# A Mamba and mixture-of-experts layer on one core: two sums of h*C in place of one, three buffers of h, and some steps moved

## The reference

```python
h = layernorm(x) * (1 + ca) + sa
z = h @ W_in;  val, gate = split(z)
val = silu(conv3(val))                      # depthwise over tokens, 3 taps, zero padding
B, C = val @ W_B, val @ W_C                 # 16 states
Delta = softplus((val @ W_delta + base) @ W_tau)
dA = Delta * A;  A_bar = exp(dA);  B_bar = expm1(dA) / (dA + 1e-6) * Delta * B
h_t = A_bar_t * h_{t-1} + B_bar_t * val_t   # for each of 512 channels and 16 states
y_t = sum over states of h_t * C_t
x = x + ga * (y * silu(gate) @ W_out + h)
h = layernorm(x) * (1 + cb) + sb
x = x + gb * (sum over the top 2 of 8 experts of gate_e * expert_e(h) + shared(h))
```

## Time and profile before

| | us |
|---|---|
| median of 3 runs | 4693.78 (4690.15 to 4694.49) |
| profiled execution | 4706.26 |
| its span in the trace | 4704.5 |
| granted TensorE clock, mean of the span | 0.887 |

### The profile page before, as it was taken

How to read it: one execution, slowest core, us unless ns; L and a number is a source line. 1 busy time by engine, 2 the same in 40 slices (tenths; PEclk the granted TensorE clock), 3 DMA queues, 4 the chain that set the end, 5 groups by cost and what they waited for, 6 DMA issues and landing times.

```text
span 4704.5 us, 37136 instructions
## 1 busy us (share of the span) xinstructions
PE 3843.4 (82%) x9708; PEld 1610.7 (34%) x9708; DVE 4026.5 (86%) x3880; ACT 3975.7 (85%) x4410; POOL 3647.9 (78%) x2304
## 2 busy tenths in 40 slices
PE   6624423999898989999899999999899977988889
PEld 3201101334333333333333333333333333333344
DVE  1388799999999999999999999999999987887820
ACT  2688889998989898999989899989999897887811
POOL 0389988887889888888889888888898886767721
PEclk8856656999999999999999999999999988989889
DMA  4588867889888888888888888888888876657542
GB/s 133 204 237 264 235 168 201 237 237 256 236 243 235 256 243 262 228 250 253 238 253 231 253 236 256 235 265 231 249 253 236 239 207 167 188 156 196 151 132 67
DMA packets 352221, 1037.19 MB, mean 220 GB/s; under 512 B 41253, under 2 KB 44389, under 8 KB 344710
## 3 DMA queue, kind: packets, MB, share of 16 engines
q1 hardware_dynamic: 278282, 766.35, 47.9%
q0 software_dynamic: 73728, 268.47, 28.8%
HBM read 639.74 MB, written 126.51 MB: 163 GB/s over the span
## 4 chain that ended last, share of the span: by engine, by line
ACT 20%; PE 19%; issue 15%; POOL 14%; DMA 13%; DVE 10%; SPq 0%; POOLq 0%; DVEq 0%; ACTq 0%
DMA ysum<-hs 11%; PE ps L1129 7%; PE ps L1148 6%; POOL inv L1390 4%; PE ps L1099 4%; ACT inv L761 3%; POOL hs L1363 3%; ACT th L772 3%; ACT inv L754 2%; ACT inv L767 2%; DVE ps L1195 2%; ACT abar L776 2%; DVE ps L1189 2%; DVE ps L1183 2%; POOL ysum L1377 2%
## 5 line engine op out<-in xcount | busy, mean ns | idle before, releaser
L1390 POOL TENSOR_TENSOR inv<-inv,th 128x1024 f32<-128x1024 f32 x512 | 1270.5, 2481 | 153.1 <-ACT th L772 153.0
L1129 PE MATMUL ps<-hf,w1r 128*128 128x512 f32 x2304 | 1129.7, 644 | 99.6 <-DMA w1r<-in_W 60.5
L1363 POOL TENSOR_TENSOR hs<-hs,Cb 128x1024 f32<-128x1024 f32 x384 | 979.7, 2551 | 28.9 <-DVE hs L1213 12.3
L1148 PE MATMUL ps<-w2r,hid 128*128 128x512 f32 x1776 | 818.3, 608 | 0.1
L1166 PE MATMUL ps<-Brow,pick 48*128 48x512 bf16 x1024 | 341.2, 416 | 576.6 <-DVE hs L1213 575.6
L1183 DVE SCALAR_TENSOR_TENSOR ps<-ps,us 128x1024 f32<-128x1024 f32 x512 | 627.8, 1226 | 172.3 <-PE ps L1166 171.8
L1377 POOL DMA_DIRECT2D ysum<-hs x480 | 443.1, 923 | 376.3 <-DMA ysum<-hs 367.2
L754 ACT ACTIVATE inv<-nrd,kappa 128x1024 f32<-128x1024 f32 (+1 forms) x640 | 578.1, 968 | 175.5 <-DVE ps L1195 171.4
L1129 PEld LDWEIGHTS ps<-hf,w1r 128*128 128x128 f32 x2304 | 458.9, 206 | 690.0 <-issue 640.9
L1202 DVE SCALAR_TENSOR_TENSOR ps<-nrd,inv_kappa,ps 128x1024 f32<-128x1024 f32 (+1 forms) x640 | 674.9, 1073 | 15.8
L1213 DVE TENSOR_TENSOR_SCAN hs<-abar,carry,ps 128x512 f32<-128x512 f32 (+1 forms) x384 | 683.1, 1800 | 0.3
(11 more groups left out here) (155 smaller groups left out, 5014.4 us busy)
## 6 DMA issues: line engine op xcount, KB each, us to landing
ysum<-hs POOLq DMA_DIRECT2D x512, 512.0 KB, 5.6
Cb<-c_rows SPq DMA_DIRECT2D x384, 512.0 KB, 4.6
w1r<-in_W SPq DMA_DIRECT2D x144, 512.0 KB, 5.6
w2r<-w_scaled SPq DMA_DIRECT2D x141, 512.0 KB, 7.3
Cb<-c_rows SPq DMA_DIRECT2D x128, 256.0 KB, 3.9
gbc<-expert_gates SPq DMA_DIRECT2D x128, 256.0 KB, 5.2
aw<-in_W_val SPq DMA_DIRECT2D x64, 256.0 KB, 6.3
xa<-in_x SPq DMA_DIRECT2D x32, 512.0 KB, 7.6
```

What stands on the lines that cost most here:

```text
L1129: mm = t.matmul(o, w1r[:, n % 2, k, h * P:(h + 1) * P], hf[:, k, :], start=(k == 0), stop=(k == G - 1))
L1148: mm = t.matmul(o, hidden(e)[:, h, tt * P:(tt + 1) * P], (last_w2(e) if q == NQ - 1 and grp == 1 else w2r[:, e % 3])[:, h, :], start=(grp ...
L1363: gp_.tensor_tensor(hs[:, c % 4, :], hs[:, c % 4, :], Cb[:, c % 2, :], ALU.mult).then_inc(hC_done, 1)
L1390: gp_.tensor_tensor(inv[:, c % 6, :], inv[:, c % 6, :], th[:, c % 3, :], ALU.mult).then_inc(thinv_done, 1)
```

## The change

It has eight parts.

1. `ysum` gets two tiles: even states add to the one, odd states to the other, each with a semaphore of its own. A sum now waits for the one two states before.
2. `add_to_y(c - 1)` stands right behind `times_C(c - 1)`, ahead of everything else of POOL's slot, but for r = 1 and 17, where it stays last.
3. `gate_y` adds the two tiles (a new POOL instruction, 128 x 1024) before it multiplies by the gate.
4. `hs` has three buffers in place of four; the scan of c waits for the sum of c - 3.
5. The edge columns of the convolution: ACT evicts all 512 columns in one activation, and DVE adds the neighbours' values with one `tensor_tensor` per block on a strided view (128 x 4 x 2), behind the four convolutions. The Silu waits for it.
6. At r = 3 DVE runs the fourth convolution ahead of the add of an expert sum (L1252) and not behind it.
7. SP loads expert p = 8 (`load_w1(qf, 8)`) at r = 23 in place of 24.
8. SP loads the gated y of a block at r = 2 in place of 3, but for the last four blocks.

```diff
-        hs = sb("hs", [P, 4, TB])
-        ysum = sb("ysum", [P, TB])
+        hs = sb("hs", [P, 3, TB])
+        ysum = sb("ysum", [P, 2, TB])
...
-            if r == 3 and has(qf):
+            if r == (2 if qf < NQ - 4 else 3) and has(qf):
                 sp.wait_ge(gy_st, 16 * units_before_end(qf))
                 ge(sp, f_gates, qf)
                 sp.dma_start(gyin, ...).then_inc(gy_ld, 16)
...
-            if r == 24:
+            if r == 23:
                 load_w1(qf, 8)
...
-                        s.activation(uu[:, m, 1:T - 1], o[:, 1:T - 1], ACT.Identity, scale=middle).then_inc(ev_val, 1)
-                        s.activation(uu[:, m, 0:1], o[:, 0:1], ACT.Identity, scale=middle,
-                                     bias=vhalo[:, m, q:q + 1]).then_inc(ev_val, 1)
-                        s.activation(uu[:, m, T - 1:T], o[:, T - 1:T], ACT.Identity, scale=middle,
-                                     bias=vhalo[:, m, NQ + q:NQ + q + 1]).then_inc(ev_val, 1)
+                        s.activation(uu[:, m, :], ps[:, bank_of["val", q, m], :], ACT.Identity,
+                                     scale=tapc[:, 1, m:m + 1]).then_inc(ev_val, 1)
...
             def silu_of_u(q):
-                    act.wait_ge(conv_done, G * (q + 1))
+                    act.wait_ge(edges_done, q + 1)
...
-                    if c >= 4:
-                        dve.wait_ge(y_summed, 16 * (c - 3))
+                    if c >= 3:
+                        dve.wait_ge(y_summed[(c - 3) % 2], 16 * ((c - 3) // 2 + 1))
...
             def late():
+                if r == 3:
+                    convolve(qa, 3)
                 if r in (2, 3, 4, 5):
                     add_x1("w2", qp, 12 * qp + 8 + r - 2, mm_w2, ev_w2)
-                if r == 3:
-                    convolve(qa, 3)
+                if r == 3 and has(qa):
+                    dve.wait_ge(conv_done, G * (qa + 1))
+                    ends = uu[:, :, 0:T:T - 1]
+                    v.tensor_tensor(ends, ends, vhalo[:, :, qa:NQ + qa + 1:NQ], ALU.add).then_inc(edges_done, 1)
...
             def add_to_y(c):
                     pool.wait_ge(hC_done, c + 1)
-                    if c % N == 0:
+                    if c % N < 2:
                         ge(pool, y_gated, unit(c))
-                        gp_.dma_start(ysum[:], hs[:, c % 4, :]).then_inc(y_summed, 16)
+                        gp_.dma_start(ysum[:, c % 2, :], hs[:, c % 3, :]).then_inc(y_summed[c % 2], 16)
                     else:
-                        pool.wait_ge(y_summed, 16 * c)
-                        gp_.dma_start(ysum[:], hs[:, c % 4, :], accum_op=ALU.add).then_inc(y_summed, 16)
+                        pool.wait_ge(y_summed[c % 2], 16 * (c // 2))
+                        gp_.dma_start(ysum[:, c % 2, :], hs[:, c % 3, :], accum_op=ALU.add).then_inc(y_summed[c % 2], 16)
...
             def gate_y(u):
-                    pool.wait_ge(y_summed, 16 * N * (u + 1))
+                    for odd in range(2):
+                        pool.wait_ge(y_summed[odd], 16 * (N // 2) * (u + 1))
+                    gp_.tensor_tensor(ysum[:, 0, :], ysum[:, 0, :], ysum[:, 1, :], ALU.add).then_inc(y_joined, 1)
+                    pool.wait_ge(y_joined, u + 1)
                     pool.wait_ge(gate_ld, 16 * (u + 1))
-                    gp_.tensor_tensor(gy[:], ysum[:], gy[:], ALU.mult).then_inc(y_gated, 1)
+                    gp_.tensor_tensor(gy[:], ysum[:, 0, :], gy[:], ALU.mult).then_inc(y_gated, 1)
...
             times_C(c - 1)
+            if r not in (1, 17):
+                add_to_y(c - 1)
...
             weight(c + 2)
             if r in (1, 17):
                 gate_y(c // N - 1)
-            add_to_y(c - 1)
+                add_to_y(c - 1)
```

More of the change, by code:

```diff
@@ L386, in adaln_mamba_moe @@
             sem("B_ready"), sem("uB_done"), sem("abar_plus_1_done"), sem("weighted_done"), sem("bu_done"), sem("scan_done"))
-        y_summed, y_gated, carry_done = sem("y_summed"), sem("y_gated"), sem("carry_done")
+        y_summed = [sem("even_states_summed"), sem("odd_states_summed")]
+        y_joined, y_gated, carry_done = sem("y_joined"), sem("y_gated"), sem("carry_done")
         a_stat, a_log, a_rstd, a_shift, a_xn = (
             sem("a_stats"), sem("a_log_variance"), sem("a_rstd"), sem("a_shift"), sem("a_normalized"))
-        tap_left, conv_done, b_split = sem("tap_left"), sem("conv_done"), sem("b_split")
+        tap_left, conv_done, edges_done, b_split = sem("tap_left"), sem("conv_done"), sem("conv_edges_done"), sem("b_split")
         ax_ld = [sem("a_x_loaded_0"), sem("a_x_loaded_1")]
@@ L846, in take_val @@
                         act.wait_ge(mm_val, G * q + m + 1)
-                        o, middle = ps[:, bank_of["val", q, m], :], tapc[:, 1, m:m + 1]
-                        s.activation(uu[:, m, 1:T - 1], o[:, 1:T - 1], ACT.Identity, scale=middle).then_inc(ev_val, 1)
-                        s.activation(uu[:, m, 0:1], o[:, 0:1], ACT.Identity, scale=middle,
-                                     bias=vhalo[:, m, q:q + 1]).then_inc(ev_val, 1)
-                        s.activation(uu[:, m, T - 1:T], o[:, T - 1:T], ACT.Identity, scale=middle,
-                                     bias=vhalo[:, m, NQ + q:NQ + q + 1]).then_inc(ev_val, 1)
+                        s.activation(uu[:, m, :], ps[:, bank_of["val", q, m], :], ACT.Identity,
+                                     scale=tapc[:, 1, m:m + 1]).then_inc(ev_val, 1)
             def diagonal(q):
@@ L1209, in scan @@
                     dve.wait_ge(bu_done, c + 1)
-                    if c >= 4:
-                        dve.wait_ge(y_summed, 16 * (c - 3))
+                    if c >= 3:
+                        dve.wait_ge(y_summed[(c - 3) % 2], 16 * ((c - 3) // 2 + 1))
                     for cols, g in parts(u):
-                        ins = v.tensor_tensor_scan(hs[:, c % 4, cols], abar[:, c % 4, cols], X(c)[:, cols],
+                        ins = v.tensor_tensor_scan(hs[:, c % 3, cols], abar[:, c % 4, cols], X(c)[:, cols],
                                                    0.0 if begins(u) else carry[:, g, c % N:c % N + 1], ALU.mult, ALU.add)
@@ L1264, in convolve @@
                     o = ps[:, bank_of["val", q, m], :]
-                    dve.wait_ge(ev_val, 3 * i)
+                    dve.wait_ge(ev_val, i)
                     v.scalar_tensor_tensor(uu[:, m, 1:T], o[:, 0:T - 1], tapc[:, 0, m:m + 1], uu[:, m, 1:T], ALU.mult,
@@ L1359, in times_C @@
                         gp_.tensor_copy(carry[:, g:g + n, c % N:c % N + 1],
-                                        hs[:, c % 4, :].rearrange("p (g t) -> p g t", g=n)[:, :, TB // n - 1:TB // n]).then_inc(carry_done, 1)
+                                        hs[:, c % 3, :].rearrange("p (g t) -> p g t", g=n)[:, :, TB // n - 1:TB // n]).then_inc(carry_done, 1)
                         pool.wait_ge(carry_done, carries(c))
                     if len(parts(u)) == 1:
-                        gp_.tensor_tensor(hs[:, c % 4, :], hs[:, c % 4, :], Cb[:, c % 2, :], ALU.mult).then_inc(hC_done, 1)
+                        gp_.tensor_tensor(hs[:, c % 3, :], hs[:, c % 3, :], Cb[:, c % 2, :], ALU.mult).then_inc(hC_done, 1)
                     else:
-                        both = hs[:, c % 4, :].rearrange("p (g t) -> p g t", g=2)
+                        both = hs[:, c % 3, :].rearrange("p (g t) -> p g t", g=2)
                         gp_.tensor_tensor(both, both, Cb[:, c % 2, 0:T].unsqueeze(1).broadcast_to([P, 2, T]),
```

## The result

The changed kernel takes 4716.2 us (median of 4, 4710.6 to 4726.9) against 4692.6 before: a ratio of 1.0056, with an interval of 1.0041 to 1.0070. It is slower by 0.56%, where 1.3% faster was forecast (60 us of 4694). The profiled execution has a span of 4725.1 us, 20.6 more than before.

The account below looks back on a forecast made before the run. DVE sets the pace, with POOL a second pacemaker for a third of each window. Terms 57 + 7 + 6 + 6 - 3 - 13 = 60 us took the median from 4693.8 to 4634 us; range 4595 to 4678, 8 in 10.

Parts of the forecast that it names:

- It keeps pace, and falls behind only at r = 1 and 17: POOL's slot of 7.6 us against DVE's 7.55; at those two places it falls some 3 us behind.
- the lag of 2 us: POOL's assumed delay behind DVE's scan; with 5.7 us landing the sum needs 10.6 of 20.3 us, so it is hidden.
- The prediction's own signs: Among them: product within 3 us of its scan at r = 24; wrong if scans wait above 20 us for sums.
- Load, 57 us: Loading p = 8 a slot earlier ends DVE's wait at r = 27: gain of 4.8 us in each of 12 windows.
- the 5.6 that the prediction allowed: Latest load issue, in us behind the end of the scan of r = 23, before the 1.4 us margin is eaten.
- Three buffers, 3 us: Cost of scans waiting for the sum of c - 3: 3 us in all, up to 58 if all landings were longest.
- if the lag stayed at 9: Three-buffer case with POOL 9 us behind: sums need 17.6 to 23.6 us, up to 3.3 us late.
- rival (d): Third buffer makes sums land late at r = 24 to 31 and unit starts: slower, likely 4735 us; chance 0.06.
- Early part, -6 us: From 235 to 470 us, where POOL is the pacemaker, 6 us of DVE's waits come back.
- Edge columns, 13 us: Cost of DVE's new instruction, partly standing behind POOL's: 0.8 us in each of 16 blocks, range 3 to 40.
- (b): Stall at r = 26 goes but DVE stops elsewhere, half given back: 25 us gained, 4669 us; chance 0.16.
- Rival (a): POOL was the true pacemaker, so all of DVE's listed waits go: capped at -95, 4599 us; chance 0.13.

Follow-up runs that it names:

- POOL relieved: Kernel before with the load of p = 8 at r = 23 and POOL's gate product at r = 22 to 24 cut to one column: 4669.5 us.
- the order with less lag: Changed kernel without edge columns, sum ahead of the weight, last beside the folds: 4666.1 us; with the load back at r = 24, 4700.1.
- the one-input form: Changed kernel with its edge columns added by eight one-column `tensor_scalar` in place of one `tensor_tensor`: 4704.0 us.

## Why the prediction was wrong

**The step that failed** is "It keeps pace, and falls behind only at r = 1 and 17", and with it the lag of 2 us in the sum for the three buffers. POOL's lag at r = 27 is 9.2 us. Two things made it, and neither stood in the prediction:

- *POOL's wait for ACT at r = 21*: 2.8 of the 4.1 us by which the lag grows in that slot. The prediction said that ACT does not set the pace. On the average of a window it does not; here `th` came at about the same time whether POOL was late or not. So POOL, which was only 2.3 us behind at r = 21, was 6.4 behind at r = 22, nearly as late as in the kernel before (7.2).
- *POOL's slot*: summed as 7.6 us from product, extra work, weight and issue. That is right for a slot without a copy of the carry and without the early issue (7.56 measured). The copy, 0.53 us in half of the windows, stood in the trace of before (288 such copies) and was left out. The wait for the product's own end was not foreseen, though the change puts the issue behind the one instruction it waits for: 0.4 to 0.6 us from start to start. The slot takes 8.2 to 8.5 us against DVE's 7.5, and from r = 22 to 27 this adds another 2.8 us.

The prediction's own signs say the same: the product was to start within 3 us of its scan at r = 24 and starts 7.9 us behind it, and DVE's scans wait for sums for more than 20 us. Three other terms turned, the first two by this lag:

- *Load, 57 us.* The stall went as worked out (4.3 us in each of 12 windows, 52). That was in part luck: SP issued the load 6.1 to 6.3 us behind the end of the scan of r = 23, not 4.2, which is beyond the 5.6 that the prediction allowed, and the transfer took 3.5 to 4.2 us and not 10.1. The two errors cancelled. The stall's end was not worth 52 us: alone it brought 3 us, within its error. I had read r = 27 as two costs side by side, while POOL needed the pause. The waits for the weight just ahead of the pause were the sign: in 11 of 12 windows the weight was late there, and behind the pause it lay ready, 2.7 to 5.2 us ahead of DVE, about what the pause had given. POOL relieved gives 21 us, and the order with less lag 34: the term depends on what is next, and I had priced only the half that was in front.
- *Three buffers, 3 us.* The kernel's scans waited 32.8 us, and with one tile and the late sum the third buffer costs 42. The formula was right (20.3 us against lag + 2.3 + 0.6 + landing) and even the case "if the lag stayed at 9" stood in it, but both inputs moved: the lag was 9.2, and the landing 8.3 on the median in place of 5.7. Two things that go with the long landings can be sorted in the traces (475 to 4120 us). In the changed kernel 387 of 443 sums were issued within 1 us of the load of a row of C, which waits for the same product: they took 8.2 us on the median, the others 4.9. And with the last sum still in flight they took 8.5, else 6.9. In the order with two tiles and the sum last, where few are issued beside the row of C, the numbers are 7.6 and 5.5. So both count, the meeting with the row of C and the second sum in flight that rival (d) named; no run separates them.
- *Early part, -6 us.* It became +6.9: POOL is the pace there and pays the 0.30 in each slot. Late issue gave 291.3 us in one kernel, and 293.4 against 299.7 in the other.

**Edge columns, 13 us.** The mechanism was right, the size too small: 20.6 us in 16 instructions, 21 to 25 us of time in the two orders with an earlier sum, and 6 with one tile and the sum last, where 13 of the 16 met nothing. The prediction took 0.8 us each, with POOL busy in half of the cases or a little more and half an instruction left; it was 1.29 on average, since 11 of the 16 stood behind a POOL instruction, for 0.2 to 2.8 us. In the longest, 2.94 us, DVE stood through the end of one POOL instruction and the whole of the next. The rule of the Trainium skill, "SBUF — State Buffer", section "Who interferes with whom", on two SBUF inputs, is borne out by these instances and by the one-input form, which never stood.

**Of the rivals**, (d) named what happened, scans that wait for late sums under a third buffer, though at 130 us where the run with it shows 42; and (b) had the gain given back at other places, though not at these. Each had less than 0.2 of the chance, and both were priced as if they came one at a time. Rival (a) was nearer to the truth of the kernel before than the forecast: POOL was a pacemaker for r = 22 to 31. But that spoke against the change, which gives POOL 32 joins of 2.36 us, 76 us, and 110 us of waits for its own product, and not for it.

**What stays open**: the +0.8 us at r = 20 and +0.6 at r = 5 and 6, waits for PE's broadcast, which vary from kernel to kernel; and why the edge columns cost 25 us in the one order with an instruction of 20.6. No run moved ACT's `th` forward at r = 21, and none had two tiles with four buffers, so what either is worth is not known.

## What to carry to other kernels

A stall at one place may be the pause in which a second engine catches up: before pricing its removal, look at how late that engine is there (start of its work behind the end of what it needs), and sum up its slot with every instruction, the small copies too, and ask what it will wait for once it is no longer late. Here it was an engine of which the average said that it had room. Taking a buffer away trades a wait that nobody feels for one on the engine that sets the pace; check its slack with the lag and the landing that the new order will have. In a chain of small issues, put between an instruction and the DMA that waits for it one piece of other work: the order that does so was 17 us faster here.

## What the runs showed of the hardware that was not expected

- DVE's `tensor_tensor` with both inputs in SBUF, 0.17 us on eight columns when POOL was idle, stood until POOL's `tensor_tensor` was through. This made 1.35 us on the median and 2.94 at most; with the sum last it was 4.48 once, where POOL ran two instructions back to back and DVE stood through both. The `tensor_scalar` instructions with one tile and a per-partition scalar took 199 to 215 ns each, all 128.
- A DMA issue on POOL directly behind the `tensor_tensor` it waits for started 0.30 us after that one's end in most of 336 cases (0.33 on average); with other work between them there was no such wait.
- A 512 KB sum took 8.3 us from issue to landing on the median when it was issued behind the product, together with the load of a row of C, and 5.7 in the kernel before.
- After PE had stood for 4.6 us for the weights, 16 matmuls took 10.2 us where they take 7.1, at a granted clock of 0.71.
